# Routed experts of a transformer block: three batches sorted as two groups instead of one

## The chip, the cores and the metric

The kernel runs on one core of one Trainium2 chip. The metric is the device time of one execution in microseconds, as the median over runs. A profiled execution gives the span, which is a little shorter than the device time, and the trace.

## What is computed

The input is x of 4 batches x 512 tokens x 128 channels. The block is attention with relative-position bias (16 heads of 64), then a mixture of experts, both gated by a modulation from c. The second half is what matters here:

```
h = layernorm(x) * (1 + cb) + sb
probs = sigmoid(h @ router_w.T + expert_bias)         # 160 experts
top_w, top_idx = top_k(probs, 8)                      # normalised, x 2.5
h1 = silu(einsum('th,eih->eti', h, w_gate))           # 64 wide per expert
routed = einsum('eti,ehi->th', h1 * combine, w_down)  # only 8 of 160 weights are not zero
x = x + gb * (routed + shared expert of h)
```

## The kernel before

Everything is float32. The attention walks over 4 batches x 8 head pairs. The order on each engine is written out by hand, and semaphores join the engines. After that the experts follow in two forms.

**Sorted experts for batches 0, 1 and 2.** Each token has eight experts. `rank`, `set_bases`, `place` and `destinations` work out, for every token and expert, a row in the DRAM tensor `sorted_rows`. This tensor consists of blocks of 128 rows, and all rows of a block belong to one expert. The first 160 blocks are known: block e belongs to expert e. What doesn't fit goes to further blocks, whose owner is found at run time (`find_owners`, `copy_owners`). For 1,536 tokens the worst case needs 95 of these, rounded up to 96. POOL scatters the tokens to their rows by indirect DMAs (`scatter`, 32 per batch, 128 tokens each): those of batches 0 and 1 between the normalisations of the attention, those of batch 2 after it. Beforehand SP fills the tensor with zeros, 1 MB per DMA (`fill`, 16 of them, by the table `FILLS`).

A *step* handles 8 blocks, so there are 32: 20 with known blocks, whose weights lie in SBUF (`known_weights`), and 12 with further blocks, whose weights SP loads expert by expert (`load_chosen`, 8 DMAs of 96 KB, 4 buffers). For a step SP loads the 8 blocks (`load_blocks`, 512 KB, into `x_blocks` in the memory of wT, 6 buffers); TensorE transposes them (`transpose_blocks`, L973), ACT and DVE copy half each (L1256, L1960), TensorE multiplies by the gate weights (`gate`, L995), ACT takes the SiLU (L1261), TensorE multiplies by the down weights (`down`, L1013), ACT and DVE copy half each (L1274, L1973), and ACT stores the blocks over their own inputs (`store_blocks`, L1282). On TensorE the order of a step is gate(s), transposes(s+1), down(s-1).

At the end POOL gathers the eight rows of each token, one tile of 128 tokens at a time (L1365, 12 tiles x 8 indirect DMAs, 6 buffers in `picked`), and DVE sums them with their weights (`combine`, L1981 to L1988).

**Dense experts for batch 3.** All 160 experts are computed for its 512 tokens, two experts as a *pair*, 80 pairs: one gate matmul over 512 columns (L1028), SiLU on ACT (L1235), multiplication by the routing weights on DVE (`weigh`, L1794), one down matmul which adds up in PSUM (L1035). The routing weights of two pairs are spread over the partitions by two DMAs of SP (`load_spread`). 12 pairs run ahead of the steps (`IN_FRONT`), 68 behind them beside the gathers.

The order around the change is this. SP, ahead of the steps:

```
            sp.wait_ge(s_scatter, 16 * TILES * TOPK)
            for s in range(NX):
                load_blocks(s)
```

and on TensorE:

```
            dense_pairs(range(IN_FRONT))
            transpose_blocks(0)
```

POOL's gathers begin when all 32 steps are stored. On DVE the combine of a tile stands between `weigh` calls, and the last two come after the fourth batch's x is ready.

## Time and profile before

| | us |
|---|---|
| median of 3 runs (lowest, highest) | 886.17 (885.7, 889.22) |
| the profiled execution | 884.65 |
| its span | 882.3 |

| engine | busy us | share of the span |
|---|---|---|
| TensorE (matmul) | 772.5 | 88% |
| VectorE (DVE) | 557.8 | 63% |
| ScalarE (ACT) | 462.5 | 52% |
| GpSimd (POOL) | 543.9 | 62% |

The durations of the profile are from one execution; the span runs from its first to its last instruction. A busy share is a mean over stages that differ, so it says little by itself: the stages are the attention (to about 530 us), routing of the last batches and the shared experts (to 573), then what is described above. In the rows further down, an arrow in brackets names who ended the idle time before an instruction. A float32 matmul over 512 columns appears as two instructions.

### The profile page before, as it was taken

The page shows a single profiled execution, that of the slowest core. Times are in us where ns is not written, and L with a number is a line of the kernel's source. Part 1 is how long each engine was busy: PE and PEld are TensorE (multiplying, and loading weights), DVE is VectorE, ACT ScalarE, POOL GpSimd, SP SyncE. Part 2 cuts the span into 40 slices and gives each one's busy share as a digit, 9 for nine tenths or more (in the row PEclk, how much of TensorE's full clock was granted, in tenths as well). Part 3 has the DMA queues.
Part 4 walks back from the last instruction along what each step waited for, and adds up shares of the span by engine and source line. Part 5 has one row for each costly group of instructions (what it writes and reads, how often), then busy time and mean ns, then how long its engine had stood idle before and what let it go on. Part 6 is the DMA issues. An engine that isn't in the chain of part 4 may idle for free.

```text
span 882.3 us, 14148 instructions
## 1 busy us (share of the span) xinstructions
PE 772.5 (88%) x4386; PEld 491.7 (56%) x4386; DVE 557.8 (63%) x1394; ACT 462.5 (52%) x965; POOL 543.9 (62%) x418
## 2 busy tenths in 40 slices
PE   4789999999989999989999987795988778799993
PEld 2556666666666666656656545434866564343441
DVE  5876766777677787777887777433433333466666
ACT  3666666666666556767667770332543334233331
POOL 0488888888877787778775782761000003777774
PEclk9899999999999999999999998897998999899997
DMA  6986958675647656446345568676998886688882
GB/s 219 241 214 189 247 138 227 199 206 138 150 120 211 195 137 177 114 102 156 90 112 129 175 210 326 227 219 243 368 381 301 293 275 207 144 189 189 188 196 57
DMA packets 81017, 174.19 MB, mean 197 GB/s; under 512 B 12448, under 2 KB 30432, under 8 KB 78640
## 3 DMA queue, kind: packets, MB, share of 16 engines
q1 hardware_dynamic: 70000, 143.59, 58.2%
q0 software_dynamic: 6144, 12.60, 5.4%
q10 hardware_dynamic: 4800, 17.11, 5.0%
q8 instruction: 36, 0.59, 0.3%
q14 instruction: 37, 0.30, 0.1%
HBM read 96.83 MB, written 45.48 MB: 161 GB/s over the span
## 4 chain that ended last, share of the span: by engine, by line
PE 42%; POOL 15%; DVE 12%; issue 11%; ACT 10%; DMA 5%; SPq 4%; POOLq 0%; DVEq 0%; ACTq 0%
POOL wT L1365 12%; PE ps L655 10%; PE ps L642 9%; ACT prob L1102 5%; PE ps L631 4%; POOL sorted_rows L1323 4%; PE ps L633 4%; PE ps L605 3%; DVE prob L1481 3%; DMA wT<-sorted_rows 3%; PE ps L973 2%; PE ps L1013 2%; SPq L490 2%; PE ps L995 2%; PE ps L668 2%
## 5 line engine op out<-in xcount | busy, mean ns | idle before, releaser
L1307 POOL TENSOR_SCALAR prob<-prob,rinv 128x512 f32<-128x512 f32 x215 | 336.1, 1573 | 102.4 <-DVE rinv L1499 99.7
L1102 ACT ACTIVATE prob<-prob,nmax 128x512 f32<-128x512 f32 x256 | 183.0, 716 | 151.4 <-DVE nmax L1481 151.0
L1365 POOL DMA_INDIRECT wT<-sorted_rows,dest x96 | 104.6, 1090 | 170.9 <-DMA sorted_rows<-prob 142.0
L1481 DVE CUSTOM_DVE_ANT_0 prob<-ps,strips 128x512 f32<-128x512 f32 x256 | 164.8, 680 | 1.2 <-PE ps L633 0.6
L642 PEld LDWEIGHTS ps<-ident,prob 128*128 128x128 f32 x1024 | 115.3, 141 | 79.3 <-POOL prob L1307 37.8
L345 DVE COPY PT<-ps 128x512 f32<-128x512 f32 x128 | 88.1, 688 | 112.4 <-PE ps L642 110.9
L642 PE MATMUL ps<-ident,prob 128*128 128x128 f32 x1024 | 137.5, 277 | 6.1 <-ACT PT L345 5.4
L655 PE MATMUL ps<-PT,v_sb 128*64 128x512 f32 x512 | 123.8, 605 | 13.0 <-ACT PT L345 13.0
L631 PE MATMUL ps<-stack 128*128 128x512 f32 x256 | 114.1, 446 | 6.7 <-DVE nmax L1481 6.4
L1323 POOL DMA_INDIRECT sorted_rows<-xn,dest x96 | 97.8, 1019 | 34.0 <-issue 34.0
L1235 ACT ACTIVATE strips<-ps 128x512 f32<-128x512 f32 x80 | 47.8, 597 | 102.5 <-PE ps L1028 102.4
L345 ACT COPY PT<-ps 128x512 f32<-128x512 f32 x128 | 73.7, 576 | 11.8 <-PE ps L642 11.3
L1960 DVE COPY v_sb<-ps 128x512 f32<-128x512 f32 x32 | 22.1, 691 | 79.3 <-PE ps L973 79.2
L655 PEld LDWEIGHTS ps<-PT,v_sb 128*64 128x64 f32 x512 | 31.1, 136 | 73.4 <-issue 50.3
L973 PE MATMUL ps<-ident,wT 128*128 128x128 f32 x256 | 38.2, 296 | 25.9 <-DMA wT<-sorted_rows 25.9
L631 PEld LDWEIGHTS ps<-stack 128*128 128x128 f32 x256 | 48.5, 189 | 21.5 <-DVE nmax L1481 14.2
L605 PE MATMUL ps<-hcur,wT 128*128 128x512 f32 x192 | 51.0, 402 | 3.6 <-DVE hcur L1420 3.6
L633 PE MATMUL ps<-k_low,stack 128*128 128x512 f32 x128 | 50.6, 395 | 0.0
L633 PE MATMUL ps<-hT,stack 128*128 128x512 f32 x128 | 50.2, 392 | 0.0
L973 PEld LDWEIGHTS ps<-ident,wT 128*128 128x128 f32 x256 | 30.1, 150 | 33.3 <-DMA wT<-sorted_rows 30.1
L1794 DVE TENSOR_TENSOR strips<-strips,qk 128x512 f32<-128x512 f32 x40 | 27.3, 694 | 33.0 <-ACT strips L1235 31.2
L1102 ACT ACTIVATION_READ_ACCUMULATOR prob<-prob,nmax 128x1 f32 x256 | 47.8, 187 | 0.0
(269 smaller groups left out, 1144.2 us busy)
## 6 DMA issues: line engine op xcount, KB each, us to landing
stack<-qk SPq DMA_DIRECT2D x128, 256.0 KB
sorted_rows<-in_zero_rows SPq DMA_DIRECT2D x16, 1024.0 KB, 5.6
wT<-sorted_rows SPq DMA_DIRECT2D x32, 512.0 KB, 5.5
sorted_rows<-prob ACTq DMA_DIRECT2D x22, 512.0 KB, 5.0
qk<-comb_rows SPq DMA_DIRECT2D x40, 256.0 KB, 4.7
strips<-in_expert_rows SPq DMA_DIRECT2D x96, 96.0 KB, 3.7
k_low<-qk SPq DMA_DIRECT2D x64, 128.0 KB
hT<-qk SPq DMA_DIRECT2D x64, 128.0 KB
```

The source lines that it names most:

```text
L345: return copy(dst[:, :, qt * P:(qt + 1) * P], ps[:, BANK_T + u % 2, :].rearrange("p (k s) -> p k s", s=P))
L605: last = nc.tensor.matmul(ps[:, BANK_PROJ + part, :], wT[:, a, part * H * HD + hp * P:part * H * HD + (hp + 1) * P], hcur[:, m, :], start= ...
L631: nc.tensor.matmul(ps[:, BANK_S + g % 2, :], stack[:, par, head, 0, qt * P:(qt + 1) * P], stack[:, par, head, 1, :], start=True, stop=False)
L633: nc.tensor.matmul(ps[:, BANK_S + g % 2, :], stack[:, par, head, 0, qt * P:(qt + 1) * P], kLow[par][:, head, :], start=False, stop=True).t ...
L642: last = nc.tensor.transpose(ps[:, BANK_T + u % 2, kb * P:(kb + 1) * P], prob[:, u, kb * P:(kb + 1) * P], ident[:, :])
L655: last = nc.tensor.matmul(ps[head * HD:(head + 1) * HD, BANK_O, :], v_sb[:, (n // 2) % 2, kb, (n % 2) * P + head * HD:(n % 2) * P + (head ...
L973: last = nc.tensor.transpose(ps[:, XT[half], j * P:(j + 1) * P], x_blocks[:, r, 4 * half + j, :], ident[:, :])
L1102: nc.scalar.activation(prob[:, u, :], prob[:, u, :], ACT.Exp, bias=nmax[:, u:u + 1], scale=-1.0, accum_out=rsum[:, u:u + 1]).then_inc(s_ex ...
L1307: nc.gpsimd.tensor_scalar(prob[:, u, :], prob[:, u, :], rinv[:, u:u + 1], None, ALU.mult).then_inc(s_prob, 1)
L1323: nc.gpsimd.indirect_dma_start(sorted_rows, bass.IndirectOffsetOnAxis(ap=dest[:, n, k:k + 1], axis=0), rows[:, n, :], None).then_inc(s_sca ...
L1365: nc.gpsimd.indirect_dma_start(picked[:, n % NGATHER, k, :], None, sorted_rows, bass.IndirectOffsetOnAxis(ap=dest[:, n, k:k + 1], axis=0)) ...
L1481: nc.vector.tensor_tensor_reduce(out=prob[:, u, :], in0=ps[:, BANK_S + u % 2, :], in1=backwards, scale=-1.0, scalar=3.0e38, op0=ALU.add, o ...
```

## The change

Batches 0 and 1 form one group with its own tensor, batch 2 a second one. The worst case needs 64 further blocks for 1,024 tokens and 32 for 512, so the groups have 28 and 24 steps, 52 in all, and each group goes through all 20 known steps. The further steps stay 12 (8 and 4).

- SP loads the first blocks as soon as the scatters of group 0 are done, ahead of the last known weights; for the first block of group 1 it waits for the scatters of batch 2. There are 26 fills: ten more, in the attention of batches 2 and 3. `x_blocks` has 4 buffers, `picked` 2.
- No pair runs ahead. From step 2 on, each step carries the gate of one pair and the down of the one before it; 50 pairs run so, 30 behind the steps. The SiLU of a pair is written back to its PSUM bank, and DVE reads it there. Among the steps all pairs use one bank, so the next gate waits for the weighing.
- POOL gathers group 0 when its 28 steps are stored. The eight combines stand in the DVE order at steps 34, 36, 39, 42, 44, 47, 49 and 51. Of the second group's four, three stand behind pairs 61, 68 and 75, the last at the end.
- The ranking of batch 2 no longer counts batches 0 and 1. The bases of batch 2 are one copy, and `rank`, `sum_blocks` and `blocks_before` have fewer matmuls for it.

```diff
-SORTED = 3
-EXTRA = -(-worst_extra(S * SORTED) // STEP) * STEP
+GROUPS = ((0, 1), (2,))
+EXTRA = tuple(-(-worst_extra(S * len(g)) // STEP) * STEP for g in GROUPS)
...
-NX, NCHOSEN, NY, NGATHER = 6, 4, 3, 6
+NX, NCHOSEN, NY, NGATHER = 4, 4, 3, 2
...
-IN_FRONT = 12
+ALONE = 2
+BEHIND = NSTEPS - ALONE
+COMBINED = (34, 36, 39, 42, 44, 47, 49, 51)
+BETWEEN = (BEHIND + 11, BEHIND + 18, BEHIND + 25)
...
             def load_blocks(s):
...
+                if s == GROUP_STEPS[0]:
+                    sp.wait_ge(s_scatter[1], 16 * len(GROUPS[1]) * SCATTERS)
+                sp.dma_start(x_blocks[:, s % NX, :, :], block_rows[g][:, first:first + STEP, :]).then_inc(s_x[s % NX], 16)
...
             sp.wait_ge(s_pv, B * HPAIRS)
-            for k in range(4, 12):
+            for k in range(4, 8):
+                load_known(k)
+            sp.wait_ge(s_scatter[0], 16 * len(GROUPS[0]) * SCATTERS)
+            for s in range(NX):
+                load_blocks(s)
+            for k in range(8, 12):
                 load_known(k)
...
-            sp.wait_ge(s_scatter, 16 * TILES * TOPK)
-            for s in range(NX):
-                load_blocks(s)
...
+                if s >= ALONE + 2 and s % 2 == 0:
+                    load_spread(next(spreads))
+                for k in range(1, CHOSEN_STEPS):
+                    for part, blocks in enumerate((range(0, 3), range(3, 6), range(6, 8))):
+                        if s == CHOSEN[k] - 7 + part:
+                            load_chosen(k, blocks)
...
# TensorE
-            dense_pairs(range(IN_FRONT))
             transpose_blocks(0)
             for s in range(NSTEPS):
                 gate(s)
...
                 if s >= 1:
                     down(s - 1)
+                if s > ALONE:
+                    dense_down(s - 1 - ALONE)
+                if s >= ALONE:
+                    dense_gate(s - ALONE)
...
# ScalarE
-                nc.scalar.activation(dense[p % NDENSE], ps[:, DENSE_BANKS[p % 3], :], ACT.Silu).then_inc(s_dsilu, 1)
+                inner = ps[:, dense_bank(p), :]
+                nc.scalar.activation(inner, inner, ACT.Silu).then_inc(s_dsilu, 1)
...
# GpSimd
-            for r in range(NY):
-                pool.wait_ge(s_y[r], 16 * len(range(r, NSTEPS, NY)))
             for n in range(TILES):
+                g = group_of(n // QT)
+                if n == QT * GROUPS[g][0]:
+                    for r in range(NY):
+                        pool.wait_ge(s_y[r], 16 * len(range(r, sum(GROUP_STEPS[:g + 1]), NY)))
                 if n >= NGATHER:
                     pool.wait_ge(s_fin, n - NGATHER + 1)
...
# VectorE
                 if s >= 1:
                     copy_results(s - 1)
+                if s >= ALONE:
+                    weigh(s - ALONE)
                 beside(s)
...
-            for n in picks:
+            for n in range(TILES - 1, TILES):
                 combine(n)
```

TensorE in the middle of the steps, before: transposes of the next step (L973), down of the last one (L1013), gate (L995), for two steps.

```order
L973 MATMUL ps<-ident,wT 128x128 x8
L1013 MATMUL ps<-strips,oT 128x128 x8
L995 MATMUL ps<-v_sb,strips 64x128 x8
L973 MATMUL ps<-ident,wT 128x128 x8
L1013 MATMUL ps<-PT,oT 128x128 x8
L995 MATMUL ps<-v_sb,PT 64x128 x8
```

The same place now, also two steps; the lines are now L1002, L1042 and L1024, and L1068 and L1061 are the down and the gate of a dense pair.

```order
L1002 MATMUL ps<-ident,wT 128x128 x8
L1042 MATMUL ps<-prob,oT 128x128 x8
L1068 MATMUL ps<-strips,stack 128x512
L1061 MATMUL ps<-yT,stack 128x512
L1024 MATMUL ps<-v_sb,prob 64x128 x8
L1002 MATMUL ps<-ident,wT 128x128 x8
L1042 MATMUL ps<-strips,oT 128x128 x8
L1068 MATMUL ps<-strips,stack 128x512
L1061 MATMUL ps<-yT,PT 128x512
L1024 MATMUL ps<-v_sb,hT 64x128 x8
```

Between the down of one step and the gate of the next stand two matmuls over 512 columns which stood outside the steps before.

VectorE at the end of the steps, before: copies of transposed blocks (L1960) and of results (L1973), then the weighing of pairs (L1794).

```order
L1960 COPY v_sb<-ps 128x512
L1973 COPY prob<-ps 128x4x128
L1960 COPY v_sb<-ps 128x512
L1973 COPY prob<-ps 128x4x128
L1960 COPY v_sb<-ps 128x512
L1973 COPY woT<-ps 128x4x128
L1973 COPY prob<-ps 128x4x128 x2
L1794 TENSOR_TENSOR strips<-strips,k_low 128x512 x2
```

VectorE in the second group now: the copies are L1986 and L1999, the weighing is L1820, and L2007 to L2014 are one combine.

```order
L1999 COPY prob<-ps 128x4x128
L1820 TENSOR_TENSOR strips<-ps,qk 128x512
L2007 TENSOR_TENSOR strips<-wT,wts 128x1024
L2011 TENSOR_REDUCE strips<-strips 128x128
L2012 TENSOR_TENSOR strips<-strips 128x128
L2014 TENSOR_TENSOR x_all<-x_all,strips 128x128
L1986 COPY v_sb<-ps 128x512
L1999 COPY prob<-ps 128x4x128
L1820 TENSOR_TENSOR strips<-ps,qk 128x512
L1986 COPY v_sb<-ps 128x512
L1999 COPY woT<-ps 128x4x128
```

A weighing stands in every step, and in eight of the steps the four operations of a combine stand between it and the copy of the next transposed blocks.

## Rows read from the trace of the kernel before

**Rows 1.** the page, part 1: TensorE's busy us, share and instructions, with the others

```profile
PE 772.5 (88%) x4386; PEld 491.7 (56%) x4386; DVE 557.8 (63%) x1394; ACT 462.5 (52%) x965; POOL 543.9 (62%) x418
```

**Rows 2.** the page, part 4: the chain that ended last, by line

```profile
POOL wT L1365 12%; PE ps L655 10%; PE ps L642 9%; ACT prob L1102 5%; PE ps L631 4%; POOL sorted_rows L1323 4%; PE ps L633 4%; PE ps L605 3%; DVE prob L1481 3%; DMA wT<-sorted_rows 3%; PE ps L973 2%; PE ps L1013 2%; SPq L490 2%; PE ps L995 2%; PE ps L668 2%
```

**Rows 3.** timeline (start, us, engine, line, op): second batch's last scatter; first dense pair

```profile
533.78 0.97 POOL L1323 DMA_INDIRECT sorted_rows<-xn,dest  x1 [0.30 <-issue]
...
573.17 2.84 PE L1028 MATMUL ps<-yT,stack 128*128 128x512 f32 x6
```

**Rows 4.** timeline: first block step; last step's down; first gather

```profile
603.71 1.97 PE L973 MATMUL ps<-ident,wT 128*128 128x128 f32 x8 [9.68 <-DMA wT<-sorted_rows]
...
734.89 1.16 PE L1013 MATMUL ps<-strips,oT 64*128 64x128 f32 x16 [0.88 <-DVE prob L1973]
...
740.71 0.99 POOL L1365 DMA_INDIRECT wT<-sorted_rows,dest  x1 [142.00 <-DMA sorted_rows<-prob]
```

**Rows 5.** timeline: transposes of two steps that follow each other without a wait

```profile
640.24 1.10 PE L973 MATMUL ps<-ident,wT 128*128 128x128 f32 x8
...
643.38 1.09 PE L973 MATMUL ps<-ident,wT 128*128 128x128 f32 x8
```

**Rows 6.** waits from 603 to 737: who waited for whom, us, times, longest

```profile
PE ps L973 <- DMA wT<-sorted_rows: 25.9, 15, 9.7
...
PE ps L995 <- DMA strips<-in_expert_rows: 5.0, 4, 3.6
```

**Rows 7.** timeline: the first gathers of two tiles, eight gathers apart

```profile
856.06 1.19 POOL L1365 DMA_INDIRECT wT<-sorted_rows,dest  x1 [0.30 <-issue]
...
867.24 1.18 POOL L1365 DMA_INDIRECT wT<-sorted_rows,dest  x1 [0.30 <-issue]
```

**Rows 8.** timeline: one dense pair after its gate, and the next gate

```profile
857.48 1.02 PE L1028 MATMUL ps<-yT,strips 128*128 128x512 f32 x2
...
858.54 0.60 ACT L1235 ACTIVATE strips<-ps 128x512 f32<-128x512 f32 x1 [1.12 <-PE ps L1028]
...
859.17 0.69 DVE L1794 TENSOR_TENSOR strips<-strips,qk 128x512 f32<-128x512 f32 x1 [1.02 <-ACT strips L1235]
...
859.20 1.02 PE L1028 MATMUL ps<-yT,strips 128*128 128x512 f32 x2
```

**Rows 9.** timeline: one DVE operation of the third batch's bases

```profile
538.36 0.32 DVE L1647 TENSOR_TENSOR strips<-strips 128x160 f32<-128x160 f32 x1
```

**Rows 10.** timeline: end of the pairs, of the gathers and of the combines

```profile
866.08 2.74 PE L1035 MATMUL ps<-strips 128*128 128x512 f32 x6
...
870.36 0.69 DVE L2020 TENSOR_TENSOR x_all<-x_all,ps 128x512 f32<-128x512 f32 x1 [0.75 <-PE ps L1060]
...
873.30 0.95 POOL L1365 DMA_INDIRECT wT<-sorted_rows,dest  x1 [0.30 <-issue]
...
875.83 1.22 DVE L1981 TENSOR_TENSOR strips<-wT,wts 128x1024 f32<-128x1024 f32 x1 [1.08 <-DMA wT<-sorted_rows,dest]
...
879.32 0.29 DVE L1988 TENSOR_TENSOR x_all<-x_all,strips 128x128 f32<-128x128 f32 x1
```

**Rows 11.** timeline: two gates of the pairs with a combine between them

```profile
851.45 1.02 PE L1028 MATMUL ps<-yT,strips 128*128 128x512 f32 x2
...
854.05 1.02 PE L1028 MATMUL ps<-yT,strips 128*128 128x512 f32 x2
```

**Rows 12.** timeline: SP issues the eight loads of a step of chosen weights

```profile
573.96 8.20 SPq L491 DMA_DIRECT2D strips<-in_expert_rows  x8
```

**Rows 13.** windows: us; busy us by engine; granted clock, DMA share, GB/s

```profile
533.00:573.00 40.00, 29.15 (x150) 18.89 (x146) 25.04 (x76) 9.50 (x14) 19.51 (x20) 0.87 0.74 265
...
640.00:670.00 30.00, 25.82 (x327) 21.62 (x324) 11.08 (x17) 14.43 (x25) 0.00 (x0) 1.00 1.03 376
...
740.00:870.00 130.00, 118.96 (x267) 50.36 (x266) 80.11 (x107) 38.80 (x65) 100.96 (x94) 0.97 0.76 172
```

**Rows 14.** longest of TensorE's waits in the attention, 220 to 533

```profile
PE ps L655 <- ACT PT L345: 10.1, 11, 1.8
```

More of the change, by code:

```diff
@@ L65, with group_of, first_of @@
 TILES = QT * SORTED
-EXTRA = -(-worst_extra(S * SORTED) // STEP) * STEP
-BLOCKS = E + EXTRA
-KNOWN_STEPS, CHOSEN_STEPS = E // STEP, EXTRA // STEP
-NSTEPS = KNOWN_STEPS + CHOSEN_STEPS
-CHOSEN = [4 + 5 * k // 2 for k in range(CHOSEN_STEPS)]
-def step_blocks():
-    known, chosen = iter(range(0, E, STEP)), iter(range(E, BLOCKS, STEP))
-    return [(next(chosen), True) if s in CHOSEN else (next(known), False) for s in range(NSTEPS)]
+GROUPS = ((0, 1), (2,))
+EXTRA = tuple(-(-worst_extra(S * len(g)) // STEP) * STEP for g in GROUPS)
+BLOCKS = tuple(E + extra for extra in EXTRA)
+KNOWN_STEPS, CHOSEN_STEPS = E // STEP, sum(EXTRA) // STEP
+GROUP_STEPS = tuple(blocks // STEP for blocks in BLOCKS)
+NSTEPS = sum(GROUP_STEPS)
+CHOSEN = (5, 8, 11, 14, 17, 20, 23, 26, 32, 38, 43, 48)
+def group_of(b):
+    return 0 if b in GROUPS[0] else 1
+def first_of(b):
+    return [a for a in GROUPS[group_of(b)] if a < b]
+def step_blocks():
+    steps = []
+    for g in range(len(GROUPS)):
+        known, chosen = iter(range(0, E, STEP)), iter(range(E, BLOCKS[g], STEP))
+        for _ in range(GROUP_STEPS[g]):
+            of_chosen = len(steps) in CHOSEN
+            steps.append((g, next(chosen) if of_chosen else next(known), of_chosen))
+    return steps
 STEPS = step_blocks()
-NX, NCHOSEN, NY, NGATHER = 6, 4, 3, 6
+NX, NCHOSEN, NY, NGATHER = 4, 4, 3, 2
 LATE = (0, 1, 2, 3, 14, 15, 16, 17)
@@ L468, in _ @@
                 stack_pair(B - 1, n + 2)
+                fill(B - 1, n)
             for at in (0, 4):
@@ L746, in rank @@
                                  skip_group_check=True)
-                for tile in [masks[a][:, 0, :] for a in range(b)] + [masks[b][:, t, :] for t in range(2 * half)]:
+                for tile in [masks[a][:, 0, :] for a in first_of(b)] + [masks[b][:, t, :] for t in range(2 * half)]:
                     nc.tensor.matmul(both, ones[:, :], twice(tile), start=False, stop=False, skip_group_check=True)
@@ L1297, in _ @@
             store_blocks(NSTEPS - 1)
-            for p in range(IN_FRONT, PAIRS):
+            for p in range(BEHIND, PAIRS):
                 dense_silu(p)
@@ L1611, in count_blocks @@
                 to = fresh[b].rearrange("p h n -> p (h n)")
[L1612 removed]
+                if not first_of(b):
                     nc.vector.tensor_copy(to, counts).then_inc(s_fresh, 1)
                     return
[L1615 to L1620 removed]
+                had = fresh[0].rearrange("p h n -> p (h n)").bitcast(F32)
+                nc.vector.tensor_tensor(to, counts, had, ALU.subtract).then_inc(s_fresh, 1)
             def sum_masks(b):
@@ L1882, in pair @@
                     match_weights(before)
-                elif before >= 0 and n == 6:
+                elif before == 0 and n == 6:
                     sum_masks(before)
@@ L1998, in beside @@
                     match_weights(2)
-            for p in range(IN_FRONT):
-                weigh(p)
+                elif s in COMBINED:
+                    combine(COMBINED.index(s))
             copy_transposed(0)
@@ L2007, in _ @@
                     copy_results(s - 1)
+                if s >= ALONE:
+                    weigh(s - ALONE)
                 beside(s)
             copy_results(NSTEPS - 1)
-            picks = iter(range(TILES))
-            for p in range(IN_FRONT, PAIRS):
+            for p in range(BEHIND, PAIRS):
                 weigh(p)
-                if p >= 21 and (p - 21) % 6 == 0:
-                    combine(next(picks))
+                if p in BETWEEN:
+                    combine(QT * GROUPS[1][0] + BETWEEN.index(p))
             dve.wait_ge(s_ddown, PAIRS)
```

176 lines of the change are left out of this document (78 added, 98 removed).

## The prediction, made before the changed kernel ran

> **What bounds the kernel now.** I read the page first: TensorE is busy 88% of the span [rows 1], but the chain that ended last has another leader, POOL's gathers of L1365 with 12%, plus the SP queue and block loads [rows 2]. So the time after the attention has several limits, and I read it as stages.
>
> Stage one, to 573 us, is attention and routing; the change touches little of it. Stage two is 12 dense pairs on TensorE beside the third batch's scatters, then a gap. The last scatter of the second batch is issued at 533.78, yet no block step starts before 603.71 [rows 3, 4], because SP waits for all 96 scatters. Stage three is the 32 block steps, from 603.71 to the end of the last down at 736.05: 132.3 us, 4.14 each. An unblocked step is 3.14 (640.24 to 643.38) [rows 5]; the surplus of 1.0 is mostly TensorE waiting for blocks (25.9 us) and for chosen weights (5.0) [rows 6]. Stage four is 96 gathers, one tile of eight each 11.18 us (856.06 to 867.24) [rows 7], beginning at 740.71, 4.7 us after the last down [rows 4]. The 68 remaining pairs run beside them. A pair takes 1.72 us of TensorE (857.48 to 859.20) [rows 8], 117 us for 68, so POOL sets this stage's end, not TensorE.
>
> **The change, part by part.** Every TensorE term is at full clock; the measured rows above are all at the 2.4 GHz level.
>
> *Steps added.* Three batches in one group need 32 steps. Two groups need 28 and 24, because each pays the 20 steps of known blocks: 52. The added 20 steps cost TensorE 20 x 3.14 = 62.8 us. No row of the change lets them be cheaper, since in an unblocked step the three groups of matmuls follow each other without a pause. This is the term against which all gains stand.
>
> *Pairs woven in.* From step 2 on each step carries one pair: 50 pairs, 30 stay behind. A step with a pair is 3.14 + 1.72 = 4.86 us on TensorE. The pair's SiLU (0.60) and its weighing (0.69) [rows 8] fall beside matmuls. They work out of PSUM now and in place, for which no row of before exists. The nearest rows are SiLU out of PSUM and the 0.69 of the weighing. I take them unchanged; even at double they are covered, since a pair's down comes 3.1 us after its gate and needs about 1.5.
>
> *Start of the steps.* TensorE's first free moment is 573.17, where the first dense pair starts now [rows 3]. The third batch becomes the first of its group, so DVE loses six operations of 160 columns at about 0.32 in the bases [rows 9] and a few in the counts, the placing and the owners: 3.7 us at most. TensorE loses some matmuls in the same chain. Not all of the chain runs through them, so between 0 and 3.7 I take 2.0: the first transposes start at 571.2. The blocks are there by then, as their loads are issued after the second batch's scatters, near 537.
>
> *Length of the steps.* Filling: transposes and copies 2.1, step 0 3.1, step 1 3.14, step 2 with a gate alone 4.0. Then 48 x 4.86 = 233.3. Step 51, without transposes, and the last down: 5.0. The sum is 250.6, so the last down would end at 821.8 if nothing waited.
>
> *Combines among the steps.* Eight tiles are combined on DVE within the second group's steps. One combine is 3.78 us (875.83 to 879.61) [rows 10]. It starts once the weighing is done, 1.5 us into the next step (the gate of 857.48 takes half a pair, so to 858.34; its weighing ends at 859.86) [rows 8], ends at 5.3, and the copy queued behind it at 6.0. The next gate wants that copy at 4.86 and starts near 6.1: 1.2 us lost, eight times, 9.6. In the pairs of before, a combine costs TensorE 0.88 (851.45 to 854.05, less 1.72) [rows 11]; that is the low bound, 7 us.
>
> *Loads.* SP issues a step of chosen weights in 8.2 us [rows 12]; at most one such step in three, with block and spread loads, this stays under 4.86 per step. For the 16 DMA engines I count bytes. A step loads and stores 1.05 MB. Chosen weights add 0.22 MB per step of group one and 0.13 in group two; a pair's rows 0.26; the gathers 0.17 in group two. At the saturated rate of the steps, 376 GB/s at a share of 1.03, and at 172/0.76 = 226 GB/s for pair rows and gathers [rows 13], a step needs 4.55 us in group one and 5.07 in group two, against TensorE's 4.86 (plus 0.4 for combines in group two). So they nearly tie. Low bound: nothing waits, 0. High bound: the ratio of before, 4.14 over its own demand of 3.57 (1.34 MB at 376), 1.16 times these demands, which is the second rival. I take 7 us, nearer the low end, because a period of 4.86 gives a load 1.7 us more than now.
>
> The gathers of group one were 64 x 1.4 us at the end and now run beside steps, but their 4.2 MB run on the same 16 engines as the step's loads. The Trainium skill, DMA: Bandwidth & Descriptors, section on issuing engines not being separate DMA queues, says the same of all issuers: they interleave, and only issue time is saved. The skill's section "Where 436 GB/s comes from" on that page puts the limit to HBM at about 358 GB/s for a core; the trace moved 376, so the measurement decides. By 358 for all bytes a step of group two would need 4.5 us, nothing would wait, and the sum would be 7 us less.
>
> *Fills.* 26 fills of 1 MB instead of 16, in the attention of the third and fourth batch. TensorE's waits there are for ACT and DVE, with none for a DMA though such fills run beside the first batches [rows 14]. I cost them at nothing; the cover is the stack buffers loaded ahead. If it failed, ten fills of 1.05 MB at 376 GB/s, 28 us of DMA time, would be the ceiling, but only the stack loads right behind one could feel it.
>
> *Tail.* After the last down: one dense down 0.86, 30 pairs 51.6, three combines at 0.88 make 55.1. From the end of the pairs to x of the fourth batch 2.23 (868.82 to 871.05), then the last combine, which stands behind it on DVE, 3.78, then 2.7 to the end of the span (879.61 to 882.3) [rows 10]. That is 63.8. The gathers of the last group need 4.7 + 31 x 1.4 + 2.5 (873.30 to 875.83) = 50.5, so they are ready before the 57.3 at which that combine starts.
>
> **Sum.** 571.2 + 250.6 + 9.6 + 7 + 63.8 = 902.2, against a span of 882.3: 19.9 longer. The profiled execution took 884.65, which is 1.5 under the median of 886.17. So 904.6 for such an execution, 906 as a median: 2.3% slower. Where the gain goes: the tail shrinks from 146.2 us after the last down to 63.8 and the 32.5 us of pairs and gap ahead of the steps vanish, together 115. But the steps grow from 132 to 267. To break even the last down would have to end by 818.5, and even without a wait it ends at 821.8.
>
> **Rivals.**
> *No waits (12%).* Loads and combines hide wholly. 821.8 + 61.2 = 883.0, 887 as a median: no change. For it: steps at 640 us run without a pause. Against it: the arithmetic of DVE above, and 31 us of load waits in the steps of before.
> *The DMA engines set the step (14%).* 1.16 x 4.55 and 1.16 x 5.07 give 5.28 and 5.88: 148 + 141 us. 571.2 + 2.1 + 289 + 63.8 = 926, 930 as a median. For it: shares of 1.03 now. Against it: pair rows are charged at a rate that was perhaps not their limit.
> *Gathers come late (8%).* This is the change not doing what it says. With two slots a tile's gather waits for the combine two before it; combines stand 2.4 steps apart, 11.9 us, a tile needs 11.2 plus landing. If a gather needed 1.7 us instead of 1.4 beside the steps, each tile would be about 1.6 us late, DVE would wait in order and TensorE behind it: 13 us more, 919.
> *Faster (4%).* The stretch before the steps holds 10.9 us of idle TensorE (40 less 29.15) [rows 13]. If the shortened chain removed 8.9 of it and the steps had no wait, the last down would end at 812.9, the time would be 878. It decides if steps start before about 567. Against it: the chain ends with the fourth batch's experts, which the change leaves alone.
>
> **Numbers.** My case has 60%; its own range is 896 to 914, from the bounds of start, combines and loads. A measurement of this kernel tells about 0.5% from no change, 881.7 to 890.6. Slower: 60 + 14 + 8 and 2 for mixtures, 84%; same 12%; faster 4%. The range from 886 to 926 takes in the case without waits and most of the upper ones.
>
> **What would show it.** TensorE near 835 us busy. First transposes of a block near 571, 52 sets of stores, the last near 838. Steps without a load wait 4.86 apart; a gate after a combine about 1.2 late, waiting for DVE's copy. No wait of SP for scatters of the third batch. A last gather some 50 us after the last down, and the chain led by TensorE. It would be wrong if steps with pairs took under 4.7 us, if load waits summed to over 25 us, or if attention grew.

## The result, and the profile after

The changed kernel took **909.88 us** in the median of 4 runs (907.45 to 915.45), the kernel before 887.69 us beside it: a ratio of 1.0258, 95% interval 1.0215 to 1.0302. It is slower, by a little more than the 2.3% forecast, and inside the range.

The profiled execution has a span of 908.1 us, where the sum gave 902.2. Part 1 of its page, the first line of part 4 (the chain that ended last) and two groups of part 5:

```profile
PE 834.9 (92%) x5154; PEld 534.8 (59%) x5154; DVE 580.7 (64%) x1422; ACT 496.0 (55%) x1025; POOL 530.3 (58%) x418
...
PE 30%; DVE 7%; issue 1%; ACT 1%; DVEq 0%; ACTq 0%
...
L1399 POOL DMA_INDIRECT wT<-sorted_rows,dest x96 | 92.5, 963 | 204.0 <-DMA sorted_rows<-prob 144.4
...
L1267 ACT ACTIVATE ps<-ps 128x512 f32<-128x512 f32 x80 | 46.4, 582 | 105.1 <-PE ps L1061 100.7
```

TensorE is busy 62.4 us more than before [rows 1], nearly the 62.8 that twenty added steps were to cost. By the list of groups, the matmuls of the steps are 60.4 of it (113.8 before, 174.2 now), the pairs 3.6, and the rest is 1.6 less. GpSimd's gathers are gone from the chain that ended last, where they led with 12% [rows 2]; the chain listed here covers the last 39% of the span. SiLU in place in PSUM takes 0.58 us, against 0.60 into SBUF [rows 8].

The step, in which most of the time lies. Timeline of TensorE, 630 to 637 us (start, us, engine, line, operation, count): gate, transposes, down, then the pair's two matmuls.

```profile
630.65 1.09 PE L1024 MATMUL ps<-v_sb,PT 128*64 128x128 f32 x16
631.67 1.09 PE L1002 MATMUL ps<-ident,wT 128*128 128x128 f32 x8
632.70 1.16 PE L1042 MATMUL ps<-strips,oT 64*128 64x128 f32 x16
633.79 1.12 PE L1068 MATMUL ps<-strips,stack 128*128 128x512 f32 x2
634.75 1.02 PE L1061 MATMUL ps<-yT,stack 128*128 128x512 f32 x2
635.70 1.09 PE L1024 MATMUL ps<-v_sb,PT 128*64 128x128 f32 x16
```

No row has idle time in brackets, and still the gates of the steps (L1024) stand 5.05 apart, not the 4.86 that a step [rows 5] and a pair [rows 8] sum to. The two dense matmuls are followed by the next group after 0.96 and 0.95 us, where a pair among pairs needs 0.86 for each.

Windows of the changed kernel (us; busy us by engine; granted clock, DMA share, GB/s): TensorE is busy without a gap up to 700 us, at a DMA share of 1.04 and 1.00, so the wait for blocks is gone.

```profile
610.00:650.00 40.00, 40.00 (x353) 26.75 (x352) 16.60 (x24) 18.65 (x32) 0.00 (x0) 1.00 1.04 330
650.00:700.00 50.00, 50.00 (x440) 33.29 (x439) 20.46 (x30) 23.10 (x40) 0.00 (x0) 1.00 1.00 315
...
780.00:840.00 60.00, 56.13 (x493) 37.31 (x494) 36.70 (x51) 25.48 (x44) 30.83 (x32) 1.00 0.81 259
```

What is left of waits is the combine. Timeline of TensorE's gates and of DVE, 746 to 753 us:

```profile
746.88 1.09 PE L1024 MATMUL ps<-v_sb,PT 128*64 128x128 f32 x16
748.21 1.22 DVE L2007 TENSOR_TENSOR strips<-wT,wts 128x1024 f32<-128x1024 f32 x1
749.46 1.92 DVE L2011 TENSOR_REDUCE strips<-strips 128x128 f32<-128x1024 f32 x1
...
751.94 0.68 DVE L1986 COPY v_sb<-ps 128x512 f32<-128x512 f32 x1
752.88 1.09 PE L1024 MATMUL ps<-v_sb,PT 128*64 128x128 f32 x16 [0.88 <-DVE v_sb L1986]
```

The copy that the next gate needs stands behind the combine on DVE; the gate comes 6.00 us after the last one, 0.95 late. This is so seven times. The eighth combine stands at the switch from the steps to the pairs, 838 to 848 us:

```profile
838.41 1.16 PE L1042 MATMUL ps<-strips,oT 64*128 64x128 f32 x16
...
839.74 1.22 DVE L2007 TENSOR_TENSOR strips<-wT,wts 128x1024 f32<-128x1024 f32 x1
...
843.47 0.68 DVE L1999 COPY prob<-ps 128x512 f32<-128x512 f32 x1
...
844.61 1.56 ACT L1267 ACTIVATE ps<-ps 128x512 f32<-128x512 f32 x3 [4.40 <-DVE prob L1999]
...
845.97 1.99 PE L1068 MATMUL ps<-strips,prob 128*128 128x512 f32 x2 [2.39 <-DVE strips L1820]
...
847.75 1.90 PE L1061 MATMUL ps<-yT,prob 128*128 128x512 f32 x2
```

DVE copies the last results only at 843.47; ACT must store them and has the SiLU of the pairs queued behind that store, so TensorE stands for 2.39 us, and its next two matmuls take 1.99 and 1.90 where 1.02 is the full-clock length: the granted clock is 0.54 from 845.9 to 849.6, nearly all at the 1.2 GHz level, behind the pause.

| stage of the profiled execution | forecast | measured |
|---|---|---|
| first transposes of a block | 571.2 | 572.86 |
| from there to the end of the last down | 267.2 (steps 250.6, combines 9.6, loads 7) | 266.7 |
| from there to the end of the span | 63.8 | 68.5 |
| span | 902.2 | 908.1 |

The middle stage came out right by luck, from errors that cancel: +9.1 for 48 pairs at 0.19, -3.0 for the combines (7 x 0.95 = 6.65, and the eighth falls into the tail), -7 for the loads, which cost nothing.

### The profile page after: what moved, and what is told of

It reads as the page before. It is cut to its first block and busy times, and to the rows that moved or that the text cites. A ratio compares the mean times of both kernels' runs of the same rounds, so it can differ in the third digit from the quotient of the medians.

```text
span 908.1 us, 15887 instructions
## 1 busy us (share of the span) xinstructions
PE 834.9 (92%) x5154; PEld 534.8 (59%) x5154; DVE 580.7 (64%) x1422; ACT 496.0 (55%) x1025; POOL 530.3 (58%) x418
## 5 line engine op out<-in xcount | busy, mean ns | idle before, releaser
L1399 POOL DMA_INDIRECT wT<-sorted_rows,dest x96 | 92.5, 963 | 204.0 <-DMA sorted_rows<-prob 144.4
L1355 POOL DMA_INDIRECT sorted_rows<-xn,dest x96 | 95.4, 994 | 36.1 <-issue 36.1
L1267 ACT ACTIVATE ps<-ps 128x512 f32<-128x512 f32 x80 | 46.4, 582 | 105.1 <-PE ps L1061 100.7
L1986 DVE COPY v_sb<-ps 128x512 f32<-128x512 f32 x52 | 35.9, 691 | 38.4 <-PE ps L1002 38.3
L1820 DVE TENSOR_TENSOR strips<-ps,qk 128x512 f32<-128x512 f32 x40 | 27.5, 690 | 50.8 <-ACT ps L1267 50.8
L1002 PE MATMUL ps<-ident,wT 128*128 128x128 f32 x416 | 56.8, 280 | 0.0
L663 PE MATMUL ps<-hT,stack 128*128 128x512 f32 x128 | 50.8, 397 | 0.0
L663 PE MATMUL ps<-k_low,stack 128*128 128x512 f32 x128 | 50.8, 397 | 0.0
L1002 PEld LDWEIGHTS ps<-ident,wT 128*128 128x128 f32 x416 | 44.5, 140 | 9.5 <-issue 9.5
L1293 ACT ACTIVATE oT<-ps 128x512 f32<-128x512 f32 x52 | 31.1, 597 | 32.8 <-PE ps L1024 32.8
```

Of the source, the lines that this page charges most:

```text
L663: nc.tensor.matmul(ps[:, BANK_S + g % 2, :], stack[:, par, head, 0, qt * P:(qt + 1) * P], kLow[par][:, head, :], start=False, stop=True).t ...
L1002: last = nc.tensor.transpose(ps[:, XT[half], j * P:(j + 1) * P], x_blocks[:, r, 4 * half + j, :], ident[:, :])
L1355: nc.gpsimd.indirect_dma_start(sorted_rows[group_of(b)], bass.IndirectOffsetOnAxis(ap=dest[:, n, k:k + 1], axis=0), rows[:, n, :], None).t ...
L1399: nc.gpsimd.indirect_dma_start(picked[:, n % NGATHER, k, :], None, sorted_rows[g], bass.IndirectOffsetOnAxis(ap=dest[:, n, k:k + 1], axis= ...
```

## The experiments

All ratios are to the kernel before on the same chip, with their 95% intervals. Differences in us are between medians, against the 909.88 of the changed kernel, which was measured in another session than the variants; the ratios are the safer comparison.

### The combines among the steps, in three pieces

```diff
                 if s >= 1:
                     copy_results(s - 1)
+                if s + 1 in COMBINED:
+                    combine_part(COMBINED.index(s + 1), 0)
+                elif s in COMBINED:
+                    combine_part(COMBINED.index(s), 1)
                 if s >= ALONE:
                     weigh(s - ALONE)
...
-                    combine(COMBINED.index(s))
+                    combine_part(COMBINED.index(s), 2)
```

Part 0 is the multiply, part 1 the reduction, part 2 the rest.

> The changed kernel with each combine among the steps split in three: product ahead of the weighing one step earlier, reduction ahead of the weighing of its step, the two short operations behind it. Theory (a combine costs because 3.8 us stand in one piece ahead of the copy that the next gate needs): seven waits of 0.95 us of gates go, and the copy of the last results is no longer 3.8 us late behind the eighth combine, which cost about 4.7 us with the half clock that followed. Together 9 to 11 us, span near 898. Rival (the steps are at TensorE's or the DMA engines' limit and the waits fill with other work): under 3 us.

Measured: 897.36 us (895.44 to 899.81), ratio 1.0118 (1.0089 to 1.0147), 12.5 us less than the changed kernel. The gates beside a combine, same view as above:

```profile
743.76 1.09 PE L1024 MATMUL ps<-v_sb,PT 128*64 128x128 f32 x16
...
747.63 1.22 DVE L2022 TENSOR_TENSOR strips<-wT,wts 128x1024 f32<-128x1024 f32 x1
748.82 1.09 PE L1024 MATMUL ps<-v_sb,PT 128*64 128x128 f32 x16
```

The period is 5.06 beside a combine too. TensorE's waits for the combines came from the order on DVE, not from the amount of DVE's work. In its profile the last down is at 829.19, from first transposes at 569.76: 259.4 us, where the changed kernel has 265.6 (838.41 less 572.86). From the last down to the end it is 65.3 against 69.7, since the pause at the switch is gone with the whole combine that stood there. These two make 10.6 us, within the 9 to 11 expected; the profile is 13.6 shorter because it also began its steps 3.1 earlier, which is scatter, as is shown below.

### The last two combines elsewhere

```diff
-COMBINED = (34, 36, 39, 42, 44, 47, 49, 51)
+COMBINED = (34, 36, 39, 42, 44, 47, 49)
...
                 weigh(p)
+                if p == BEHIND + 2:
+                    combine(len(COMBINED))
...
+            combine(TILES - 1)
             dve.wait_ge(s_ddown, PAIRS)
```

> The changed kernel with two combines moved: the eighth from step 51 to behind pair 52, the twelfth ahead of the fourth batch's result. Theory (the tail of 68.5 us instead of my 63.8 comes from the copy of the last results, late behind the eighth combine, which stops TensorE 2.4 us and halves its clock): last down to end of span falls to about 63 us, span near 903. Rival (the tail is set by the 32 gathers with two slots): last down to end stays at 68 us.

Measured: 904.89 us (903.74 to 906.32), ratio 1.0199 (1.0172 to 1.0227), 5.0 less. TensorE's pause at the switch is gone, and from the end of the last down to the end of the span it takes 64.6 us instead of 68.5, where 63 was expected and the rival had 68. So the switch costs most of what the tail was over its forecast.

### Both together

> The changed kernel with both edits on the combines: those beside steps in three pieces around the weighing (alone -12.5 us in the median), and the eighth behind pair 52, the twelfth ahead of the last result (alone -5 us). Theory (they act at different places, 746 to 835 and 840 to 908 us): they add, 909.9 - 17.5 = 892.4, 890 to 896. Rival (the last combine of the steps is the same loss in both, or the gathers on GpSimd then end last): 896 to 900.

Measured: 899.77 us (895.14 to 902.64), ratio 1.0144 (1.0106 to 1.0182). The gains don't add; within the intervals it is the split alone, whose tail (65.3 us from the last down) this kernel repeats with 65.7. The rival holds: splitting already removes the pause at the switch, and what the second edit still does is to move the twelfth combine ahead of the last result, which gives nothing back. End of its profile:

```profile
884.93 2.74 PE L1068 MATMUL ps<-strips 128*128 128x512 f32 x6
...
886.35 1.21 DVE L2007 TENSOR_TENSOR strips<-wT,wts 128x1024 f32<-128x1024 f32 x1
...
890.84 0.66 PE L1093 MATMUL ps<-ident,oT 128*128 128x128 f32 x4 [3.17 <-DVE oT L2069]
```

TensorE's last transposes now wait 3.17 for what used to follow at once: the combine has only changed places with the result.

### The gate of a pair apart from its down

```diff
+                if s >= ALONE:
+                    dense_gate(s - ALONE)
                 if s >= 1:
                     down(s - 1)
                 if s > ALONE:
                     dense_down(s - 1 - ALONE)
-                if s >= ALONE:
-                    dense_gate(s - ALONE)
```

> The changed kernel with the gate matmul of the dense pair moved between the transposes and the down group of the step, so that the pair's two matmuls no longer stand together: TensorE changes four times a step between groups of 64 columns and matmuls of 512, not twice. Theory (each such change loses about 0.1 us, which is why a step with its pair took 5.05 us and not 3.14 + 1.72 = 4.86): the step takes 5.24 us, 50 x 0.19 = +9.5 us, 917 to 921. Rival (the 0.19 us comes from the semaphore waits of the step's pieces, or from the place, not from the change of shape): the step stays at 5.05, 908 to 912.

Measured: 903.22 us (901.93 to 913.21), ratio 1.0208 (1.016 to 1.0255). The theory fell: with twice the changes of shape the step is as long.

```profile
635.45 1.02 PE L1061 MATMUL ps<-yT,stack 128*128 128x512 f32 x2
636.40 1.16 PE L1042 MATMUL ps<-PT,oT 64*128 64x128 f32 x16
637.50 1.13 PE L1068 MATMUL ps<-strips,stack 128*128 128x512 f32 x2
638.55 1.09 PE L1024 MATMUL ps<-v_sb,strips 128*64 128x128 f32 x16
639.58 1.09 PE L1002 MATMUL ps<-ident,wT 128*128 128x128 f32 x8
640.51 1.02 PE L1061 MATMUL ps<-yT,stack 128*128 128x512 f32 x2
```

5.06 from gate to gate of the pair. So the 0.19 goes with the pair in a step, whatever it stands beside. It isn't a full DMA side either: in the kernel before, matmuls of pairs follow each other after 0.86 from 857 to 860 us at a DMA share of 1.07. Why is open. That the median was nonetheless 6.7 us lower wasn't foreseen; the intervals of the two ratios overlap. SiLU and weighing of the pair now start a group earlier, so DVE reaches the combine earlier: two gates beside a combine (755.23 and 760.69) are 5.46 apart, not 6.00, seven times 0.54 or 3.8 us. The other part in its profile is a start 2.2 us earlier (first transposes at 570.66), scatter again.

### All pairs behind the steps

```diff
-ALONE = 2
-BEHIND = NSTEPS - ALONE
+ALONE = NSTEPS
+BEHIND = 0
...
-COMBINED = (34, 36, 39, 42, 44, 47, 49, 51)
+COMBINED = (36, 39, 42, 45, 49)
...
-BETWEEN = (BEHIND + 11, BEHIND + 18, BEHIND + 25)
+BETWEEN = (2, 9, 16, 23, 30, 37)
```

> The changed kernel with all 80 dense pairs behind the 52 steps (the combines then stand beside steps 36, 39, 42, 45 and 49 and beside pairs 2 to 37). Theory (two groups cost TensorE 21 more steps; the pairs between them fill the time in which the transfers of a step are under way): a step alone takes 3.14 us of TensorE but its transfers take longer, as in the kernel before, whose 31 steps took 131 to 134 us, 4.2 to 4.3 each; so 52 steps take 215 to 225 us, with waits for blocks of 50 us or more in the list of waits, 50 pairs behind cost 50 x 1.72 = 86 where 48 woven ones cost 48 x 1.91 = 92 on the path: 909.9 + 52 x 1.15 - 6 = about 960, 940 to 970. Rival (weaving hid nothing, the loads keep ahead of bare steps): 52 steps at 3.2 us, and the whole 895 to 905.

Measured: 930.84 us (920.35 to 937.67), ratio 1.052 (1.0468 to 1.0571). It lies below the range expected, far above the rival's. Weaving is worth about 20 us, not 50; its four runs spread from 920 to 938, and the profiled one is the shortest of them. A stretch of its steps, and its waits from 573 to 785 (the lines L1024 and L1984 are the gate and DVE's copy for it):

```profile
620.95 1.09 PE L1002 MATMUL ps<-ident,wT 128*128 128x128 f32 x8
624.09 1.09 PE L1002 MATMUL ps<-ident,wT 128*128 128x128 f32 x8
...
639.76 1.09 PE L1002 MATMUL ps<-ident,wT 128*128 128x128 f32 x8 [1.14 <-DMA wT<-sorted_rows]
644.31 1.09 PE L1002 MATMUL ps<-ident,wT 128*128 128x128 f32 x8 [1.33 <-DMA wT<-sorted_rows]
```

```profile
PE ps L1002 <- DMA wT<-sorted_rows: 13.6, 12, 1.9
...
PE ps L1024 <- DVE v_sb L1984: 10.7, 6, 2.2
```

Bare steps do run into their loads, at 3.14 for a while and then 4 to 5 apart. But the waits for blocks are 13.6 us where I expected 50 or more, and the 52 steps with their combines take 197 us (569.91 to the first pair at 767.2), 3.8 each. I had scaled them by the 4.14 of before. Why the loads of the kernel before came later than these is not shown.

### Light steps in the second group

The 20 known steps of the second group leave out seven of eight gate and down matmuls, and six of eight transposes (the last of each half stays). Copies, loads, stores and pairs stay.

```diff
-                for j in range(STEP):
+                for j in range(STEP - 1 if light(s) else 0, STEP):
```

> The changed kernel without 7 of 8 matmuls of each group in the 20 known steps of the second group (one or two transposes of 8, one gate and one down of 8 are left), so most results of the third batch's known blocks are not computed; all copies, loads, stores and pairs stay. Theory (TensorE alone sets the step): these 20 steps lose up to 2.6 us each, until ACT and VectorE with a combine (2.7 and 5.9 us) or the loads bound them: 25 to 45 us less, span 865 to 883. Rival (the 16 DMA engines tie with TensorE at 5.07 us or more for a step of this group, as I counted from bytes): under 10 us less, and TensorE waits for blocks instead.

Measured: 898.09 us (896.83 to 906.29), ratio 1.0152 (1.0103 to 1.02): 12 us less, for about 52 us of TensorE's work left out (of a step's 3.14 us, 7/8 of 2.11 and 3/4 of 1.03, 20 times). That is nearer to the rival's 10 than to the theory's 25 to 45. The windows show that TensorE is then idle for a fifth of the time, at a mean granted clock of 0.81 and 0.86, while the DMA engines stay full until 780:

```profile
735.00:780.00 45.00, 34.95 (x133) 16.48 (x132) 26.44 (x37) 17.27 (x33) 28.60 (x30) 0.81 1.03 343
780.00:840.00 60.00, 46.72 (x156) 22.40 (x155) 38.57 (x53) 22.28 (x41) 27.54 (x28) 0.86 0.77 240
```

Its longest waits were for DVE's copy behind a combine. With the combines in pieces as well:

> The changed kernel with the light steps of the second group (seven of eight matmuls and transposes of each group left out in 20 known steps, as in the light steps run) and with the split combines. It asks what stands behind TensorE in the second group. Theory (DVE's whole combine between the steps was what held the light steps, waits of 4.9 us at TensorE's gate): both gains add, 909.9 - 12 - 12.5 = about 885, 882 to 889. Rival (the arrival of the gathered tiles and the transfers, DMA share 1.03, pace the light steps, and a split combine waits for the tile all the same): 893 to 898.

Measured: 895.22 us (892.06 to 901.19), ratio 1.0093 (1.006 to 1.0126); the rival holds. The waits only change their name, from the order on DVE to the tiles themselves:

```profile
DVE strips L2026 <- DMA wT<-sorted_rows,dest: 20.1, 6, 8.0
...
PE ps L1002 <- DMA wT<-sorted_rows: 5.9, 3, 3.4
```

So even where the second pass over the known experts costs TensorE only about a sixth, two groups in this arrangement are not faster than the kernel before. What stands behind TensorE is transfers: gathered tiles (with their two slots) and, less, blocks. No run separates the two slots from the full DMA engines, and the lower clock has a part too: in the first of these runs TensorE's busy time fell by only 30 us (834.9 to 804.8) for the 52 left out.

### SiLU in PSUM, alone and undone

The change also leaves the SiLU of a pair in PSUM. Alone, in the kernel before (with it, not shown, DVE's weighing reads the PSUM bank, and the gate that uses the bank next waits for the weighing instead of the SiLU):

```diff
-                if p >= NDENSE:
-                    act.wait_ge(s_ddown, p - NDENSE + 1)
-                nc.scalar.activation(dense[p % NDENSE], ps[:, DENSE_BANKS[p % 3], :], ACT.Silu).then_inc(s_dsilu, 1)
+                inner = ps[:, DENSE_BANKS[p % 3], :]
+                nc.scalar.activation(inner, inner, ACT.Silu).then_inc(s_dsilu, 1)
```

> This is the kernel before with one part of the change alone: the SiLU of a dense pair is written back to its PSUM bank and VectorE reads it there. Grouping, steps and gathers are those of before. In the trace of before a gather beside the pairs took 1.40 us from start to start (11.18 us for 8), many with a duration of 1.41; in the changed kernel most gathers follow each other after 1.25. Theory (the 1.41 comes from VectorE reading two SBUF operands in the weighing while GpSimd builds a gather): gathers fall to about 1.25, 96 of them save 14 us, of which TensorE (68 pairs and 12 combines, 127 us) lets 8 to 12 through: span 870 to 875. Rival (the gathers of before were slowed by the spread loads on the same DMA engines): gathers stay at 1.40, span 882 as before.

> The kernel of the run with the SiLU in PSUM once more, word for word, for a second profile, because the first profiled execution was 4 us longer than the median of its own runs. Theory (the part's gain of 10 us lies behind 735 us, where gathers and TensorE end together): median 877 to 879, and from the last down group to the end some 8 us less than the 146.2 us of before. Rival (it lies in executions whose steps run at a lower clock before 735 us, and the end is as long as before): from the last down group to the end within 2 us of before.

> The kernel before, unchanged, for a second profile on the same chip: its profiled execution (882.3 us of span) was shorter than its median. Both theories on the SiLU in PSUM need it: the ratio is 1.00, the span 884 to 888, and the start of the first dense pair (573.17 in the first profile), the last down group (734.89) and the end show by how much the same program moves at each stage from one execution to the next. If the start of the first pair moves by 1.5 us or more, the 1.7 us by which the changed kernel's first transposes came late is scatter, not the cost of its ten more fills.

Measured: 877.78 us (877.06 to 883.59), ratio 0.9894 (0.9868 to 0.992), and in the second run 880.68 us (874.85 to 885.44), ratio 0.9926 (0.9902 to 0.995). It is faster, by 0.7 to 1.1%. The kernel before against itself gave 1.0009 (0.9986 to 1.0033). The four profiles, and that of the next section, split at the last down group:

| | first pair | last down | first to last gather | last down to end |
|---|---|---|---|---|
| before | 573.17 | 734.89 | 132.6 | 147.4 |
| before, again | 577.74 | 737.70 | 132.9 | 147.4 |
| SiLU in PSUM | 574.97 | 739.02 | 128.3 | 142.8 |
| SiLU in PSUM, again | 573.04 | 729.68 | 128.9 | 143.3 |
| and weights in PSUM, pieces | 572.73 | 736.84 | 118.9 | 133.4 |

The end is the same to 0.5 us from one profile to the next and shorter by 4.1 to 4.6 us with the SiLU in PSUM, which is what the gathers save (128.3 and 128.9 for 132.6 and 132.9). So the place was the theory's, the size half of it. Beside a weighing alone a gather took up to 1.42 us before and takes 0.94 to 0.99 now, with the spread loads unchanged, so the rival falls. Before:

```profile
780.93 0.69 DVE L1794 TENSOR_TENSOR strips<-strips,qk 128x512 f32<-128x512 f32 x1 [1.03 <-ACT strips L1235]
781.03 1.41 POOL L1365 DMA_INDIRECT wT<-sorted_rows,dest  x1 [0.30 <-issue]
```

By the medians the gain is 6 to 10 us; where the part beyond 4.6 lies, the profiles don't show. The steps ahead scatter by up to 9 us (last down at 729.68 to 739.02), which is why one profile can't show a gain of 5. The start scatters too, and it goes with TensorE's granted clock from 533 to 575. Before: 0.88 with the first pair at 573.17, 0.75 with 577.74. In the changed kernel and its variants: 0.88 with first transposes at 569.76, 570.66 and 570.78; 0.80 with 569.91 and 571.30; 0.76 and 0.77 with 572.23 to 573.46; 0.66 with 579.82 (the run below). The window of the second profile of before:

```profile
533.00:575.00 42.00, 33.24 (x145) 20.93 (x140) 24.53 (x74) 9.02 (x13) 20.99 (x21) 0.75 0.77 263
```

Undone in the changed kernel (SiLU to SBUF, weighing from there):

> The changed kernel with the SiLU of the pairs written to SBUF again, as in the kernel before, so that DVE's weighing reads two operands there; the rest of the change stays. Theory (this part paid 1.1% in the kernel before only because the gathers on GpSimd and TensorE ended together there; in the changed kernel TensorE alone sets the end): gathers beside weighings get longer (L1399 mean from 0.96 to 1.05 to 1.10 us), the time stays at 909.9, within 907 to 913. Rival (the SiLU in PSUM gains its 10 us in the changed kernel too, by shorter turns of ACT, DVE and TensorE): 917 to 921.

Measured: 909.98 us (905.76 to 919.93), ratio 1.0249 (1.0217 to 1.0281), and a mean gather of 1031 ns instead of 963, a little under the 1.05 to 1.10 us expected. The profiled execution is its longest, 919.93 us. The same part that gains in the kernel before gains nothing measurable where TensorE sets the end.

### A version that beats both

The kernel before with the SiLU in PSUM, the weights of the twelve tiles copied to a PSUM bank that is free behind the steps, and the combines in pieces.

```diff
+            wts_near = ps[:, XT[1], 0:NT * TOPK].rearrange("p (n k) -> p n k", k=TOPK)
+            then(nc.vector.tensor_copy(wts_near, wts[:, :, :]))
             for p in range(IN_FRONT, PAIRS):
                 weigh(p)
-                if p >= 21 and (p - 21) % 6 == 0:
-                    combine(next(picks))
+                n, part = divmod(p - 23, 6)
+                if n >= 0 and part < 3:
+                    (multiply_picked, reduce_product, add_reduced)[part](n)
```

> The kernel before with the SiLU of the pairs left in PSUM (alone 0.9894 of before), the twelve tiles' weights copied into a free PSUM bank so that the combine's multiply reads one operand there, and each combine in three pieces behind three pairs, from pair 23 on. Theory (a gather on GpSimd is stretched where DVE reads two operands from SBUF, and TensorE loses 0.85 us at each combine): no gather over 1.1 us beside L1983's multiply where one in eight took 1.99, gathers 1.25 apart throughout, a tile in 10.1 us instead of 11.14, and 6 pairs in 10.3: 870 us, 866 to 873. Rival (the multiply's output or its size stretches the gather, not where the weights lie): the 1.99 stays, the gathers pace the end, and it is 876 to 880.

Measured: **868.50 us** (864.83 to 872.02), ratio 0.9783 (0.9749 to 0.9816): 2.2% faster than before, and 868.50 against 909.88 for the changed kernel. The edit of the SiLU is the one shown above. Of its 18 us, 14.0 lie behind the last down (147.4 against 133.4). The weights in PSUM and the pieces were not run apart, so how the gain divides between them isn't shown; what lengthens a gather is. SiLU in PSUM alone, GpSimd and DVE beside a combine:

```profile
815.72 1.22 DVE L1983 TENSOR_TENSOR strips<-wT,wts 128x1024 f32<-128x1024 f32 x1
815.77 1.99 POOL L1365 DMA_INDIRECT wT<-sorted_rows,dest  x1 [0.30 <-issue]
```

The same in the changed kernel with the split combines (L2022 is the multiply of a combine in pieces):

```profile
803.22 1.22 DVE L2022 TENSOR_TENSOR strips<-wT,wts 128x1024 f32<-128x1024 f32 x1
803.81 1.44 POOL L1399 DMA_INDIRECT wT<-sorted_rows,dest  x1 [2.46 <-issue]
```

With the weights in PSUM, the multiply and then the reduction:

```profile
788.48 1.21 DVE L1983 TENSOR_TENSOR strips<-wT,ps 128x1024 f32<-128x1024 f32 x1
788.73 0.94 POOL L1365 DMA_INDIRECT wT<-sorted_rows,dest  x1 [0.30 <-issue]
...
790.21 1.90 DVE L1991 TENSOR_REDUCE strips<-strips 128x128 f32<-128x1024 f32 x1
791.23 0.95 POOL L1365 DMA_INDIRECT wT<-sorted_rows,dest  x1 [0.30 <-issue]
```

And all 96 of them (least, median and most ns, first and last start):

```profile
L1365 POOL DMA_INDIRECT wT<-sorted_rows,dest x96: 942/944/1061, 742.3 to 861.2; - x96
```

The order of starts decides. Where both operands of the multiply lie in SBUF, a gather that starts before it, or within 0.03 us of it, takes 0.94 or 0.95 us. One that starts later takes 1.99 at 0.05 us into the multiply, 1.83 at 0.21, 1.64 at 0.41, 1.44 at 0.59 and 1.10 at 0.93: all end about 2.0 us after the multiply's start, 0.8 after its end. The rule holds for the weighings of the kernel before too: 34 of its 96 gathers are lengthened by a product of two SBUF operands, and each ends 0.81 to 0.83 us after that product. With one operand in PSUM, eight gathers start 0.25 to 0.96 us into a multiply, and all take 0.94 or 0.95. Cutting the combine in pieces does not do this, as the 1.44 beside a cut combine with both operands in SBUF shows. The reduction, with one operand in SBUF, never lengthened a gather. The gather of 1061 ns runs beside the two short operations at a combine's end, which read two SBUF operands of 128x128.

## Why the prediction was right

**Sign and cause.** Twenty steps at 3.14 are 62.8 us of TensorE, and 60.4 were measured for the steps' matmuls (62.4 in all, where the pairs' 3.6 and the 1.6 saved elsewhere meet); against them stood 31 us of load waits [rows 6] and a tail whose gathers came off the path. The chain is TensorE's, the last gather starts 10 us before the combine that reads it, and SP waits for no scatter of the third batch: the mechanism was as told. The last gather starts 50.8 us after the last down, as forecast, but by luck: the gathers stand 1.25 apart, not 1.4, and begin 7.5 after it, not 4.7, with two waits for a free slot.

**Start, 571.2.** 572.86. In seven profiled variants, with the same code up to there, the first transposes began between 569.76 and 573.46, and in an eighth, the one with the SiLU in SBUF, at 579.82. The 1.7 are within that scatter, which goes with the clock granted in the routing stage. At the same clock of 0.88 the start is 569.8 to 570.8 against 573.17 for the first pair before: 2.4 to 3.4 us gained, where I took 2.0. The ten added fills weren't tried alone. In the profile they show no cost: TensorE has no wait of note for a DMA in the attention, whose last matmuls (L698) start at 536.6 to 539.3 in the changed kernel and three variants, against 537.7 and 538.3 (L668) before.

**Length of a step, 4.86.** 5.05 in every step with a pair: the one term that was mis-sized, +9.1 us. I had taken the pair's 1.72 from a stretch that holds pairs alone. A bare step and a pair don't sum; the run with the gate apart shows that it isn't the number of changes between shapes, which was my first explanation. The prediction's sentence that its rows are all at the 2.4 GHz level holds for those that price a step and a pair (granted clock 1.00), but not for the first transposes in [rows 4], 1.97 us where 1.10 is usual.

**Combines, 9.6.** 0.95 each where I had 1.2, with 0.88 as the low bound, and seven of them, since the eighth falls into the tail. The working of one was nearly right: a gate comes 6.00 us after the last one beside a combine, where I had about 6.1. It costs less because the step without a combine is 5.05 and not 4.86, so this miss is mostly the last one seen from the other side.

**Loads, 7.** Nothing: in the list of waits from 573 to 848 TensorE waits for no DMA, though the share is 1.04. (The only row with a DMA is GpSimd's, which waits for a group's stores before it gathers, as it should.) The trace agrees here with what followed from the 358 GB/s of the Trainium skill's "DMA: Bandwidth & Descriptors" (section "Where 436 GB/s comes from"), that nothing would wait, though not with the figure as a limit: the unwoven steps moved 392 GB/s from 575 to 610. A share near 1 said that the engines had work, not that they were late. The rival in which the DMA engines set the step (926 us) failed on this; in the light steps with split combines transfers are the longest waits.

**Tail, 63.8.** 68.5. The step that failed is the switch: I let the pairs follow the last down at once, and forgot that the eighth combine stands on DVE ahead of the last results' copy, which holds ACT's store, and this the SiLU. The rows price it at 4.5 us: waits of 0.30 and 2.39, and 1.8 for two matmuls at half the clock. Moving the eighth combine, and the twelfth with it, gave 5.0 us back.

**Break-even.** "To break even the last down would have to end by 818.5": with the split combines it began at 829.19, and that kernel is still 1.2% slower than before. None of the repairs to the order of the two groups changes the sign.

**Not foreseen at all**: that what the change did in passing, SiLU in PSUM, was worth 0.7 to 1.1% by itself in the kernel before. I had costed it at nothing because ACT and DVE were covered. The part of it that the profiles locate works through a third engine: GpSimd's gathers set the end there (the chain named them [rows 2]), and their length depends on where DVE reads.

## What to carry to other kernels

A second pass over fixed work has to be paid in full on the engine that does it; idle time elsewhere in the profile pays it back only once, and what is moved into it meets the next limit close behind. Ask of every long vector instruction what is queued behind it on its engine, and cut it where another engine's next operand stands: in pieces it cost TensorE nothing, whole 0.95 us each. And where GpSimd sets the end, look at what DVE reads at the same moment before adding or moving work.

## What the runs showed of the hardware

- An indirect gather on GpSimd took 0.94 to 1.00 us alone or beside DVE instructions with at most one operand in SBUF. One that started after DVE had begun a product of two SBUF operands ended 0.8 us after the product: 1.99 us beside one of 128x1024 begun 0.05 us earlier, 1.41 beside one of 128x512 begun 0.10 us earlier. One that had started first took 0.94 or 0.95. With one operand of the product in PSUM the effect is gone, and the 96 gathers follow each other at 1.25 us instead of 1.40.
- A 512-column matmul took 0.86 us among its like and 0.95 among the groups of 8 and 16 short matmuls of a step, whether the pair's two stood together or apart. The cause is open.
- A pause of 2.39 us on TensorE was followed by two matmuls at half the clock (1.99 and 1.90 for 1.02). In the routing stage the same program was granted 0.75 or 0.88 from one execution to the next, with starts of the next stage 4.6 us apart.
- The DMA engines showed a share of 1.04 at 330 GB/s with no consumer waiting, and moved 392 GB/s in another order of the steps.
